# A two-layer decoder kernel: the last routing steps of layer zero earlier, and the first contexts of layer one loaded during self attention

## The reference

```python
x = x + L0_attn(layernorm(x))                 # linear attention, 16 heads
x = x + L0_xattn(layernorm(x), ctx, ctx)      # cross attention, 16 heads of 16
x = x + L0_ffn(layernorm(x))
x = x + L1_attn(layernorm(x))                 # self attention, 16 heads of 64
x = x + L1_xattn(layernorm(x), ctx)           # layernorms x and ctx itself; 8 heads of 64
x = x + L1_ffn(layernorm(x))                  # 8 experts, top 2, capacity 33

def L0_ffn(x):                                # 16 experts, top 2, one shared expert
    s = sigmoid(x @ gate_w + gate_b)
    values, ids = top_k(s, 2);  values /= values.sum()
    expert = lambda x, e: (silu(x @ wg[e]) * (x @ wu[e])) @ wd[e]
    return x + expert(x, shared) + sum(values[k] * expert(x, ids[k]) for k in range(2))

def L1_xattn(x, ctx):
    cn = layernorm(ctx);  k, v = split(cn @ Wkv);  q = layernorm(x) @ Wq
    return softmax(q @ k.T / 8) @ v @ Wout + bout
```

## Time and profile before

| | us |
|---|---|
| three executions | 1847.66, 1855.84, 1855.99 (median 1855.84) |
| the profiled execution, its own time | 1852.79 |
| its span in the trace | 1851.1 |
| PE busy | 1644.8 (89%) |
| DVE busy | 1167.7 (63%) |
| ACT busy | 845.5 (46%) |
| POOL busy | 575.1 (31%) |

### The profile page before, as it was taken

One profiled execution on the slowest core, in us unless ns is written; L12 is line 12 of the kernel. 1 busy time (PEld: TensorE's weight loads), 2 busy tenths in 40 slices (PEclk: granted clock), 3 DMA queues, 4 the chain that ended last, 5 costly groups with the idle time before them and its releaser, 6 DMA issues. The chain is left out here.

```text
span 1851.1 us, 36828 instructions
## 1 busy us (share of the span) xinstructions
PE 1644.8 (89%) x12703; PEld 1358.4 (73%) x12703; DVE 1167.7 (63%) x2713; ACT 845.5 (46%) x2455; POOL 575.1 (31%) x894
## 2 busy tenths in 40 slices
PE   6997599999998785899999579999999759999988
PEld 3665377777776574788888557777777659999986
DVE  5776467777776543477776546666666446666656
ACT  2333256555554142455555434444444235544524
POOL 2112223444442253222210022232322155444413
PEclk9999699999998898999999789999999969999999
DMA  8000323444450452000000030000000031123001
GB/s 249 0 0 1 124 69 123 129 128 127 128 153 12 154 171 94 21 14 14 16 6 1 1 110 18 18 18 18 18 9 1 1 137 69 69 91 114 1 1 40
DMA packets 87274, 114.25 MB, mean 62 GB/s; under 512 B 4788, under 2 KB 76680, under 8 KB 86888
## 3 DMA queue, kind: packets, MB, share of 16 engines
q1 hardware_dynamic: 82008, 99.56, 16.8%
q0 software_dynamic: 5136, 12.98, 2.1%
HBM read 64.68 MB, written 47.84 MB: 61 GB/s over the span
## 5 line engine op out<-in xcount | busy, mean ns | idle before, releaser
L1312 PE MATMUL ps<-e_ex_high,e_w_high 128*128 128x264 f32 x512 | 146.8, 287 | 6.4 <-POOL e_w_low L2671 6.4
L1312 PE MATMUL ps<-e_ex_high,e_w_low 128*128 128x264 f32 x512 | 146.6, 286 | 0.0
L1312 PE MATMUL ps<-e_ex_low,e_w_high 128*128 128x264 f32 x512 | 146.2, 285 | 0.0
L1027 ACT ACTIVATE c_probs<-ps,c_negmax 112x375 f32<-112x375 f32 x256 | 143.5, 581 | 2.1 <-DVE c_negmax L1126 2.1
L1224 PEld LDWEIGHTS ps<-const,c_probs 112*125 112x125 f32 x768 | 97.7, 193 | 47.8 <-DVE c_pT L1142 27.5
L1126 DVE TENSOR_REDUCE c_negmax<-ps 112x2 f32<-112x750 f32 x128 | 114.2, 934 | 25.5 <-PE ps L1255 25.5
L1224 PE MATMUL ps<-const,c_probs 112*125 112x112 f32 x768 | 115.8, 288 | 3.6 <-ACT c_probs L1027 2.4
L1924 PE MATMUL ps<-xnT,s_qkv 128*128 128x224 f32 x512 | 110.5, 365 | 4.7 <-ACT e_gate_up L1717 4.2
L1733 ACT ACTIVATE s_probs<-ps,s_negmax 112x112 f32<-112x112 f32 x256 | 86.5, 364 | 36.7 <-DVE s_negmax L1791 36.7
L1312 PEld LDWEIGHTS ps<-e_ex_high,e_w_high 128*128 128x128 f32 x512 | 97.7, 191 | 6.6 <-issue 6.6
L1924 PEld LDWEIGHTS ps<-xnT,s_qkv 128*128 128x128 f32 x512 | 94.8, 193 | 10.5 <-ACT e_gate_up L1717 5.8
(11 more groups left out here) (392 smaller groups left out, 4741.7 us busy)
## 6 DMA issues: line engine op xcount, KB each, us to landing
expert_rows<-d_zero SPq DMA_DIRECT2D x16, 2240.0 KB
c_ctx_in<-in_ctx SPq DMA_DIRECT2D x32, 375.0 KB
e_x_in<-expert_rows SPq DMA_DIRECT2D x43, 128.0 KB, 2.2
expert_rows<-e_y POOLq DMA_DIRECT2D x43, 128.0 KB, 2.1
e_w_gate_even<-in_L_ffn_w_gate SPq DMA_DIRECT2D x4, 1024.0 KB, 5.1
e_w_fc_even<-in_L_ffn_w_c_fc SPq DMA_DIRECT2D x4, 1024.0 KB, 7.3
e_w_proj_even<-in_L_ffn_w_c_proj SPq DMA_DIRECT2D x4, 1024.0 KB, 9.7
e_w_gate_odd<-in_L_ffn_w_gate SPq DMA_DIRECT2D x4, 1024.0 KB, 5.0
```

What stands on the lines that cost most here:

```text
L1027: last = nc.scalar.activation(probs[:, g % 2, r, :], ps[:T, r, 0:S], ACT.Exp, bias=negmax[:, par, h:h + 1], accum_out=sums[:, par, h:h + 1])
L1312: last = nc.tensor.matmul(out, a, b, start=start and n == 0, stop=stop and n == len(pairs) - 1)
```

## The change

Three edits. (1) Behind the loop of cross attention zero the routing goes one batch further: the gate of batch 14 joins the "inverse" step, batches 12 and 13 are placed or chosen inside the last unit, the gate and the choice of batch 15 and the scatter of batch 14 come before the block's end. The shared expert's products are cut in parts around the steps. (2) `experts_0` loses one gate and one choice; the second half of its shared products comes behind the table, `multiply(0)` behind `plan`, and SP reads its registers before it waits for the scattered rows. (3) A new class `ContextEntry` loads contexts 0 and 1 at the start of self attention and normalises context 0 in its iterations 13 and 14; in cross attention one the value half of `c_kv` is split on DVE, the key half on ACT and POOL, and PE waits for both halves only at its first key product.

```diff
     def banks(self, bank):
-        side = self.sh.ps[:T, bank, :]
+        side = self.sh.ps[:T, bank, 4 * T:]
...
     def bank(self, k, n):
-        return self.sh.ps[:, 2 * k + n, 0:self.G * T]
+        return self.sh.ps[:, 2 * (1 - k) + n, 0:self.G * T]
...
     def silu(self, act, k):
-        act.wait_ge(self.up_mm, 2 * k + 2)
+        act.wait_ge(self.up_mm, 4 * k + 2)
...
     def multiply(self, dve, k):
         dve.wait_ge(self.silu_done, k + 1)
+        dve.wait_ge(self.up_mm, 4 * k + 4)
...
@@ cross attention zero, POOL, behind the loop
             dispatch.scatter(pool, B - 4, 0)
+            dispatch.total(pool, B - 3, 1)
+            dispatch.scatter(pool, B - 3, 1)
             norm_power(nc, sh, pool, ln, B)
-            dispatch.total(pool, B - 3, 1)
             dispatch.keep_own(pool, B - 1, 1, side_done, steps.before(B - 1) + len(steps.now(B - 1)) + 3)
+            dispatch.total(pool, B - 2, 0)
             dispatch.keep_rows(pool, B - 2, 0)
             dispatch.add_rows(pool, B - 1, 1, xn_ready)
-            dispatch.scatter(pool, B - 3, 1)
-            dispatch.total(pool, B - 2, 0)
+            dispatch.scatter(pool, B - 2, 0)
@@ ACT, behind the loop
-            copy_second(B * UNITS - 1)
+            copy_second(B * UNITS - 1, 0)
+            dispatch.exps(act, B - 2)
             shared.silu(act, 0)
             shared.silu(act, 1)
-            dispatch.exps(act, B - 2)
+            dispatch.exps(act, B - 1)
@@ DVE, in the last unit
+                if closing:
+                    dispatch.place_rows(dve, B - 4, 0)
+                    dispatch.choose(dve, B - 3, 1, ("sigmoid", "best", "hot"))
...
+                if closing:
+                    inverse_sums(B, 1)
@@ DVE, behind the loop
-            inverse_sums(B, 1)
-            evacuate("inverse", end, B, None)
-            dispatch.place_rows(dve, B - 4, 0)
+            evacuate("inverse_gate", end, B, None)
             scale_heads(B, end + 1)
-            shared.multiply(dve, 0)
-            dispatch.choose(dve, B - 3, 1, ("sigmoid", "best"))
+            dispatch.place_rows(dve, B - 3, 1)
+            dispatch.choose(dve, B - 2, 0, ("sigmoid", "best"))
             evacuate("result", end + 1, B, None)
             statistics(B, end + 2)
-            dispatch.choose(dve, B - 3, 1, ("hot",))
+            dispatch.choose(dve, B - 2, 0, ("hot",))
             normalise(B, 1)
+            shared.multiply(dve, 0)
+            evacuate("rows", end + 2, B, None)
             shared.multiply(dve, 1)
-            evacuate("rows", end + 2, B, None)
-            evacuate("gate", end + 3, B, None)
-            dispatch.place_rows(dve, B - 3, 1)
+            evacuate("gate", end + 3, B + 1, None)
+            dispatch.place_rows(dve, B - 2, 0)
             shared.add(dve, 0)
-            dispatch.choose(dve, B - 2, 0, ("sigmoid", "best", "hot"))
+            dispatch.choose(dve, B - 1, 1, ("sigmoid", "best", "hot"))
             shared.add(dve, 1)
@@ PE, behind the loop, from "rows" on
+            side("rows", end + 2, B, 1)
+            shared.up(pe, 1, 0, (1,))
+            shared.up(pe, 1, 1, (0,))
+            side("gate", end + 3, B + 1, 0)
+            shared.up(pe, 1, 1, (1,))
             shared.down(pe, 0)
@@ experts_0, PE
-            dispatch.gate(pe, B - 1, 1).then_inc(gate_mm, 1)
-            up(0)
-            pe.wait_ge(dispatch.logits_taken, B)
             dispatch.gate(pe, B, 0).then_inc(gate_mm, 1)
             pe.wait_ge(dispatch.totals_ready, B + 1)
             nc.tensor.matmul(ps[:T, BANK_PLAN, 0:E0], sh.c("ones")[:T, :], dispatch.totals[:, 1, :], start=True, stop=True).then_inc(counts_mm, 1)
-            up(1)
+            up(0)
             pe.wait_ge(table_ready, 1)
...
             last.then_inc(table_mm, 1)
+            up(1)
@@ experts_0, SP
             sp.wait_ge(plan_ready, 1)
+            at = loaded_values(sp, 1, 0, REGIONS * ROWS - TILE)
             for u in range(2):
                 sp.wait_ge(dispatch.scattered[u], 16 * B)
@@ self attention one
+class ContextEntry:
...
+    def load(self, sp, q, u):
+        src = self.sh.ins["ctx_1024"].rearrange("b (j p) d -> b p j d", p=KC)
+        sp.dma_start(self.ctx_in[:, u, :, :], src[q]).then_inc(self.loaded[u], 16)
+
+    def statistics(self, dve, q, u):
+        nc = self.nc
+        dve.wait_ge(self.loaded[u], q * 8 + 16 - 8 * u)
+        dve.sem_inc(self.passed, 1)
+        for j in range(NK):
+            last = nc.vector.bn_stats(self.stats[:, j, :], self.ctx_in[:, u, j, :])
...
+        for j in range(NK):
+            last = nc.vector.bn_aggr(self.mv[:, j, :], self.stats[:, j, :])
...
+    def power(self, pool, q):
+        pool.wait_ge(self.var_ready, q + 1)
+        self.nc.gpsimd.tensor_tensor(self.rstd[:, :], self.veps[:, :], self.sh.c("minus_half")[:KC, 0:NK], ALU.pow).then_inc(self.rstd_ready, 1)
+
+    def rows(self, dve, q, u):
+        nc = self.nc
+        dve.wait_ge(self.rstd_ready, q + 1)
+        for j in range(NK):
+            last = nc.vector.tensor_scalar(self.cn[:, j, :], self.ctx_in[:, u, j, :], self.mv[:, j, 0:1],
+                                           self.rstd[:, j:j + 1], ALU.subtract, ALU.mult)
+        last.then_inc(self.cn_ready, 1)
...
+        @block.sync
+        def _(sp):
+            for u in range(2):
+                entry.load(sp, u, u)
...
+                if i == B - 2:
+                    entry.power(pool, 0)
...
+                if i == B - 3:
+                    entry.statistics(dve, 0, 0)
+                if i == B - 2:
+                    entry.rows(dve, 0, 0)
@@ cross attention one
-            pool.wait_ge(kv_rounded, 1)
-            nc.gpsimd.tensor_tensor(kv_low[:, :, :], w.kv[:, :, :], kv_high[:, :, :].bitcast(F32), ALU.subtract).then_inc(kv_split, 1)
+            pool.wait_ge(kv_rounded, 2)
+            nc.gpsimd.tensor_tensor(kv_low[:, :, 0:512], w.kv[:, :, 0:512], kv_high[:, :, 0:512].bitcast(F32), ALU.subtract).then_inc(kv_split, 1)
...
+            nc.vector.tensor_copy(kv_high[:, :, 512:1024], w.kv[:, :, 512:1024]).then_inc(values_rounded, 1)
+            dve.wait_ge(values_rounded, 1)
+            nc.vector.tensor_tensor(kv_low[:, :, 512:1024], w.kv[:, :, 512:1024], kv_high[:, :, 512:1024].bitcast(F32),
+                                    ALU.subtract).then_inc(kv_split, 1)
...
                     if part == 0:
+                        if first(i + 1):
+                            pe.wait_ge(kv_split, 2)
                         pe.wait_ge(ctx_split, 2 * i + 4)
...
             pe.wait_ge(sh.w_loaded["router1"], 32)
-            pe.wait_ge(kv_split, 1)
             sequences(iteration)
```

142 lines of the change are left out of this document (66 added, 76 removed).

## The result

The changed kernel takes 1851.29 us, the median of 20 executions (1835.20 to 1857.92); the kernel before, in 20 executions beside them, 1856.47 us (1844.76 to 1861.59). The ratio is 0.9969 with a 95% interval of 0.9955 to 0.9982: 5.8 us less (3.3 to 8.4). The profiled execution took 1850.48 us, its span is 1848.8 us, 2.3 less than that of before. It was begun with a handicap: the first context's transposes of cross attention zero, in code that the change does not touch, stand at 211.74 us in it and at 209.62 before. Times after must be compared with 2.1 us taken off.

What follows compares the result with a forecast made beforehand. PE, busy 89% of the span, was taken as the bound, with gains only where it waits at joints between blocks. Terms: -6.5 - 0.9 + 1.0 = -6.4 us; from the mean 1853.1, 1847 us, range 1840 to 1856.

Steps and rivals of the forecast that it cites:

- Start of cross attention one: PE's first query there no longer waits for `kv_low` and starts 6.5 us earlier, with all behind it: -6.5 us.
- The split's margin: Cross attention one: the weights' split is done before the first key product at 1074.8, hidden by 5 us at least.
- The third context: Cross attention one: its data come just in time for the earlier statistics; bounds 0 and 1 us late, taken as 0.
- What self attention pays: At its start two context loads beside the first gather delay it by 0 to 2.2 us, taken as +1.0 us.
- The late work on DVE: Late self attention: first context's statistics (1.74 us) and rows (1.06 us) fit DVE's idle time; otherwise at most 0.6 us.
- End of cross attention zero: Reordered routing and a new DVE wait make the block end at 615.7, 1.8 us later.
- The new wait: End of cross attention zero: `multiply(1)` on DVE waits for the last up product; ranks come at about 609.5, before 607.38.
- Start of the experts: PE's own wait, no longer SP, sets the first tile: PE ready at 634.5 against 635.36, 0.9 us earlier.
- Half at the low clock: Start of the experts: first eight up products, half at the low clock, last to 5.9 us; table and plan 6.9 us.
- More: Rival, 22%: PE's clock rises earlier, two queries give 3.2 us and the experts some 1 us more: -10.6, 1842.5 us.
- The joint ahead eats it: Rival, 18%: first tile 2 us later, gather the full 2.2, third context 1 late: -1.3 us, 1852.
- Slower: Rival, 8%: the shared products run at half speed, the clock staying low through both tails: +6.6 us, 1860.

Runs made afterwards that it cites:

- split_alone: Kernel before with only the split of the key and value weights changed, contexts loaded and normalised where they were: 1858.81 us, ratio 1.0008.
- contexts_only: Kernel before with only the contexts' part: early loads, first context's rows in self attention, weights' split shared out; no routing part: 1851.06 us, ratio 0.9964.
- gate_first: Changed kernel with DVE's second shared multiplication moved behind the last gate's evacuation and the placing of batch 14 in cross attention zero: 1842.84 us, one execution.
- loads_late: Changed kernel with the two context loads issued only after self attention's first batch is through its normalisation: 1848.89 us, ratio 0.9956 to the kernel before.

## Why the prediction was right

The forecast was -6.4 us and 1847 us, the ratio gives -5.8 us and the median is 1851.29 us, inside the range of 1840 to 1856. The median is further off than the difference because my 1847 was built on a mean of four executions, 1853.1, where twenty give 1856.47. That the difference is hit so closely is in part luck: two terms of the sum are off by 2.4 and 0.3 us, and what the traces add up to is less than the times show. Step by step:

- **Start of cross attention one, -6.5: right.** From PE's last transposes of self attention to the query it was 9.60 us before (1060.52 to 1070.12) and is 3.16 after (1062.40 to 1065.56), -6.4, and H stays 11.19. The split's margin is 7.2 us (at least 5 forecast), although POOL's half took 3.00 us and not 2.25; my cast of 1.6 us was 0.69, on the safe side: the 802 ns of the earlier trace rows are a mean over 64 with one of 7.62 in it, which I did not notice; the other 63 take 0.69 in the mean. The third context is in time.
- **What self attention pays, +1.0: mis-sized.** It is 3.4 us (3.2 in this pair of traces), above my upper bound of 2.2. The step that failed is "the contexts occupy a third of the engines and not all, so I take 1.0", with a bound taken from a scatter. The gather's landing went from 1.7 to 5.1 us, though the loads' share is a third. The rule quoted from the Trainium skill (DMA: Bandwidth & Descriptors; "Queues, rings and completion order") led to an estimate of 0.4 to 0.8 us, further off still. The late work on DVE costs nothing that can be seen: split_alone, with neither it nor the old wait, and contexts_only, with it, had the same moments of the clock, and G is 332.14 and 332.32.
- **End of cross attention zero, +1.8: mis-sized.** The new wait is there as described (2.75 us idle ahead of `multiply(1)`, about 3 forecast), and the ranks come 0.9 us later than before with the handicap taken off (2.1 forecast). But A grows by only 0.8 us in the pair, and by 0.6 in the means of five and seven traces. Most of the error lies ahead of the ranks: the rows are copied 1.2 us earlier than before and not 0.5, and from there to the ranks it takes 3.68 us and not 4.2. Behind the ranks the remainder is 6.0 us (6.2 forecast, 6.5 before): the first down products start 0.8 us ahead of the ranks, the second wait only 0.78 us for the additions (2.01 before) and take 1.95 us instead of 2.64, as the granted clock no longer falls while they run. From the last addition to the next block's first instruction it is 0.4 us more.
- **Start of the experts: right in what binds, off in the middle.** "Half at the low clock" failed: all eight up products ran at 1.2 GHz, until 7.2 us behind the first instruction instead of 5.9. So the plan comes at 7.71 and not 6.9, the last addition at 15.36 and not 14.3, the registers take 1.67 and not 2.1: PE is ready after 17.03 us, 16.5 forecast. From the first context's transposes to the first tile the pair has 425.74 and 424.50, -1.2 against my -0.9; in the means of the five traces without the routing part and the five with it as changed it is 425.4 and 424.2, again -1.2. The terms, +1.8 and -2.6 us, measured +0.8 and -2.1: two errors of opposite sign.
- **The rivals.** "More": the first two queries still take 3.33 and 3.36 us. The clock rose not earlier but 3.2 us later behind the first query than before, and the third query paid 1.3 us for it in this pair. "The joint ahead eats it": its gather came true and was worse, its late tile did not. "Slower": the low clock held for one group of eight up products, 2.8 us more than at the full clock, not for both tails.

Added up by the traces: -6.4 + 3.4 - 1.2 = -4.2, inside the interval of 3.3 to 8.4 us less, on its small side. The pair of traces itself differs by 4.4 us with the handicap taken off. One candidate for the rest: PE's product behind its second reading of registers stands 20.1 to 23.5 us behind the first tile in the nine traces with the routing part and 22.3 to 24.2 in the five without, 1.7 us less in the mean. The clock has a part in it: in the five it is at half until 5.7 to 6.7 us behind the first tile, in eight of the nine it rises by 3.7 us behind it or has risen before; in the ninth, gate_first, it rises 6.5 us behind it, and that trace has the 23.5. Whether that belongs to the change, by the tile that comes sooner or by SP's earlier loads, is open.

## What to carry to other kernels

An early wait that is taken away gives only what the next one leaves: by the traces the split of the weights was worth 0.8 us alone and 6.4 us with the contexts there, so both have to move. A prefetch costs what it runs beside: place it where the transfers beside it have room, not in the first free queue slot; here the same loads 70 us later cost nothing that can be seen. And look for the same instruction with two durations before believing a mean of a group: the largest gain of this study (0.5%) came from POOL's pause in a block that nobody had touched, and what pointed to it was one stalled rounding. By J the stall accounts for 8 us in six traces of ten, the short waits beside the same run for some 3 us in each.

## What the runs showed of the hardware

- Two transfers of 375 KB from SP's queue, which by themselves keep the DMA engines busy to a share of 0.34 (loads_late, 802 to 804), delay an indirect gather of POOL, whose first transfer is issued 1.2 us behind them: F is 4.9 to 5.2 us instead of 1.7.
- A DVE rounding of 128x528 takes 0.43 to 1.05 us, but the first one in the last block takes 7.60 to 7.95 us in six of ten traces, while POOL subtracts without a gap; it ends 0.3 us behind the end of POOL's run, whether that run has 24 subtractions or 15. The Trainium skill (SBUF — State Buffer, "Who interferes with whom") says that DVE and GpSimd share a pair of ports, which a DVE cast can take in its two-port modes, and that whoever issues first gets it for the whole instruction while the other blocks. No trace shows in which mode this rounding ran. One POOL instruction lasts 0.7 us, and by that rule alone DVE would wait no longer than one; it was passed over by some ten in a row. Why four of ten traces escape is open.
- Executions of one kernel scatter by some 20 us (16.8 before, 22.7 after, over twenty each), and the traces show two sources: the stalled rounding (8 us), and the moment at which the clock falls and rises, which differs between executions. Counted from the first transposes of self attention the clock is back at the full level after 8.6 to 15.1 us; by itself that and the dip behind it are worth up to 3 us in G, and there are more such joints.
